# Loop 1 of a two-layer graph and mixture-of-experts kernel: S of two blocks by the two row halves of PE's array

## The chip, the cores and the metric

The kernel runs on one core of a Trainium2 chip. The metric is the time of one execution on the device, in microseconds; the runs are given by their median and their range. A second kind of execution is recorded by the hardware profiler, and all rows of a trace come from one such execution. Engines are called PE (TensorE), DVE (VectorE), ACT (ScalarE), POOL (GpSimd) and SP (the queue that issues most transfers).

## The reference

The input x has 5000 rows of 128; adj is a sparse 5000 x 5000 matrix of zeros and ones. Four steps follow one another, each with a layer norm ahead and a residual sum behind it. The first is the one that the change touches:

```
adj = A * (y @ y.T)                  # y: one-hot classes, 5000 x 16
row_l1 = maximum(sum(abs(adj), axis=1), 1e-12)
support = (adj / row_l1) @ input     # input = layernorm(x)
return 0.9 * support + 0.1 * h0
...
x = x + gnn0(layernorm(x)); x = x + moe0(layernorm(x))   # 8 experts, top 2, and a shared FFN
x = x + gnn1(layernorm(x)); x = x + moe1(layernorm(x))   # adj @ x and edge sums; 8 experts, top 2
```

The product y @ y.T is called S here. It is multiplied with adj, element by element, to give m.

## The kernel before

The 5000 nodes are padded to 5120, that is NB = 40 blocks of 128, or CH = 10 chunks of CW = 512 columns. Everything is ordered by hand: each engine runs its own program of nested loops over chunks k and steps s, and semaphores tie them together.

**Loop 1** (`a_iteration`, driven by `a_pipeline`) computes the first graph step, chunk by chunk. A chunk has STEPS = 43 steps. At step s of chunk k, for s below 40, PE multiplies block s of `ysta` (128 rows x 128, the stationary side) with the chunk's `ymov` (128 rows x 512) into one of two S banks, `sbank[s % 2]` (L726). DVE multiplies the bank with the adjacency block that lies in `ring` into `m` (L1561). Two steps later (LAG = 2) PE aggregates: `abank` += xn[b].T @ m[b] for b = s - 2 (L742), two instructions on PE since both sides are plain float32. ACT takes |m| into `mabs` (L1065), and once in four steps PE sums four such blocks by column quarters, `add_abs` (L790, 128 rows x 32 columns each); in chunks and loads named in PAIRS it does the same with edge products, `add_cols` (L800), after DVE made them (L1571). An S matmul waits until m of the block that last used its bank is made.

**y** has 16 classes. As float32 it is split into a high and a low part of type float32r, so that high x high, high x low, low x high and low x low give the full product. In `ysta` rows 0 to 63 hold two copies of the high part (32 rows each, of which 16 are zero), rows 64 to 127 two copies of the low part; `ymov` holds the 32-row groups in the order 0, 2, 1, 3. One contraction over 128 rows adds up all four products. `load_y` brings y in by 4 transfers for each piece, ACT makes the high part (`y_high_copy`, L959), DVE the low part on rows 64 to 127 (`y_low`, by `split_low`, L386), and `load_ymov` copies the chunk's columns from `ysta` to `ymov` by 4 transfers (L533). SP does that at the start of its loop for chunk k, that is behind the loads of chunk k-1.

**Beside these** PE runs, at fixed steps of a chunk, the transposes, router and ranks of the chunk before, and for chunks 2 to 8 the shared FFN of the chunk two before: `shared_up` at steps 2, 11, 20, 29 (three float32r matmuls into `ubank[n % 2]`, L665 to L667) and `shared_down` at steps 4, 13, 22, 31 (L680). ACT applies gelu between them.

SP loads the adjacency by 1 MB transfers of four blocks, in the order of LOAD_ORDER: `ring` slots 0, 1, 4 hold what S is multiplied with, the other slots the outgoing edges. Each load waits until its slot's last user is done. After loop 1 come the expert tiles, loop 2 (`z_iteration`, second graph step) and its expert tiles; they use the same PSUM banks, but nothing in them changes.

The eight PSUM banks are s0, s1, agg, u0, u1, d0, d1 and misc.

Of the kernel before, what the change touches and what calls it, by code (L numbers as in the profile page):

```python
# [8 lines left out]
ACT = mybir.ActivationFunctionType  # L9
# [7 lines left out]
P = 128  # L17
# [5 lines left out]
CLS = 16  # L23
# [12 lines left out]
GROUPS = P // 32  # L36

# [107 lines left out]
def bass_two_layer_gnn_moe_kernel(nc, x_t, adj_in, adj_out, h0_t, y_t, wr0, w1s, b1_0, w2s, b2_0,  # L145
# [144 lines left out]
    ubank = [psum("u0"), psum("u1")]  # L290
    dbank = [psum("d0"), psum("d1")]
# [179 lines left out]

    def beside(layer, s):

        i, q = divmod(s, TILE_STEPS[layer])
        return (layer * TILES + i if 0 <= i < BESIDE[layer] else None), q
# [26 lines left out]
    def _(sp):  # L502
# [26 lines left out]
        def load_ymov(k, buf):  # L529
            wait(sp, s_made, (k - 1) * NB)  # L530
            wait(sp, ymov_landed, 64 * k)
            for dst, src in enumerate((0, 2, 1, 3)):
                sp.dma_start(ymov[32 * dst:32 * dst + 32, buf, :].bitcast(F32),  # L533
                             ysta[32 * src:32 * src + 32, cols(k)].bitcast(F32)
                             ).then_inc(ymov_landed, 16)

        def load_y(first, last, landed):
# [3 lines left out]
            for g in range(4):  # L541
                sp.dma_start(dst[32 * g:32 * g + 32, :], y_t[:, first * YP:first * YP + n]).then_inc(landed, 16)
# [19 lines left out]
        for k in range(CH):  # L562
            if k:
                load_ymov(k, k % 2)
            for l in range(0 if k else 4, LOADS):
                load_next(2 if k and l in PAIRS[k] else 1)
# [85 lines left out]
    def _(pe):  # L652
# [5 lines left out]
        def shared_up(j, hb):  # L658
# [3 lines left out]
            wait(pe, ffn_gelu, n - 1)  # L662
            at, u = slice(hb * P, (hb + 1) * P), ubank[n % 2]
# [52 lines left out]

        def a_iteration(k, agg, mid, run_ffn):
            S, n = SA, width(k)
            for s in range(STEPS):
                if agg and s < NB:  # L720
                    if s == 0:
                        wait(pe, ymov_landed, 64 * (k + 1))
                    if isinstance(k, int) and k == 0 and s % Y_BLOCKS == 0:
                        pe.wait_ge(y_split, s // Y_BLOCKS + 1)
                    wait(pe, m_made, k * NB + s - 1)
                    pe.matmul(sbank[s % 2][:, 0:n], ysta[:, s * P:(s + 1) * P], ymov[:, k % 2, 0:n],  # L726
                              start=True, stop=True).then_inc(s_made, 1)
# [227 lines left out]
    def _(act):  # L955
        def y_high_copy(c):
            act.wait_ge(yraw_landed[min(c, 2)], 16 * 4)
# [125 lines left out]
        def shared_gelu(j, hb):  # L1083
# [4 lines left out]
            act.activation(h[:, n % H_BUFS, :], ubank[n % 2][:], ACT.Gelu, bias=b1[:, hb:hb + 1]).then_inc(ffn_gelu, 1)  # L1088
# [827 lines left out]
```

## Time and profile before

| what | us |
|---|---|
| median of 3 runs | 1473.44 |
| their range | 1466.86 to 1474.15 |
| span of the profiled execution, first to last instruction | 1555.4 |
| PE busy in it | 1367.5 (88%) |
| DVE busy | 929.2 (60%) |
| ACT busy | 649.6 (42%) |
| POOL busy | 461.5 (30%) |

For the profiled execution the span is the only time there is; it is longer than the runs without a profiler, so sums are made from its rows and then set against the median. Loop 1 reaches from about 13 us to about 735 us of the span. Start times in a row are from the span's start. Matmuls are pipelined: a row's duration has a modelled end, and two rows can overlap, so what an instruction costs PE is read from start to start. PEld rows are weight loads, which run beside the matmuls.

### The profile page before, as it was taken

The page shows a single profiled execution, that of the slowest core. Times are in us where ns is not written, and L with a number is a line of the kernel's source. Part 1 is how long each engine was busy: PE and PEld are TensorE (multiplying, and loading weights), DVE is VectorE, ACT ScalarE, POOL GpSimd, SP SyncE. Part 2 cuts the span into 40 slices and gives each one's busy share as a digit, 9 for nine tenths or more (in the row PEclk, how much of TensorE's full clock was granted, in tenths as well). Part 3 has the DMA queues.
Part 4 walks back from the last instruction along what each step waited for, and adds up shares of the span by engine and source line. Part 5 has one row for each costly group of instructions (what it writes and reads, how often), then busy time and mean ns, then how long its engine had stood idle before and what let it go on. Part 6 is the DMA issues. An engine that isn't in the chain of part 4 may idle for free.

```text
span 1555.4 us, 21717 instructions
## 1 busy us (share of the span) xinstructions
PE 1367.5 (88%) x6536; PEld 829.7 (53%) x6536; DVE 929.2 (60%) x2670; ACT 649.6 (42%) x1108; POOL 461.5 (30%) x450
## 2 busy tenths in 40 slices
PE   5998999999999999998689999999999998766771
PEld 2443444444444444456578877466666666545550
DVE  6775858576776767684322224777777777432224
ACT  3454344343444433444244344565555555422220
POOL 2102021111202020213545554223323332465652
PEclk9999999999999999999899999999999999978885
DMA  9688988696888787875366442889888888433435
GB/s 314 253 335 315 337 297 305 239 341 238 321 274 317 265 318 266 304 248 206 104 250 223 170 165 96 312 296 311 296 292 308 304 287 250 117 111 113 126 109 202
DMA packets 117360, 386.22 MB, mean 248 GB/s; under 512 B 20116, under 2 KB 49587, under 8 KB 87824
## 3 DMA queue, kind: packets, MB, share of 16 engines
q1 hardware_dynamic: 77296, 327.32, 60.9%
q10 hardware_dynamic: 27136, 33.93, 6.2%
q0 software_dynamic: 12832, 23.81, 4.3%
q8 instruction: 46, 0.75, 0.2%
q14 instruction: 50, 0.41, 0.1%
HBM read 332.80 MB, written 57.41 MB: 251 GB/s over the span
## 4 chain that ended last, share of the span: by engine, by line
PE 51%; issue 12%; DVE 10%; another core or an unknown queue 5%; ACT 4%; POOL 3%; DMA 2%; DVEq 0%; POOLq 0%; ACTq 0%; SPq 0%
PE agg L742 14%; PE d L846 7%; PE s L726 6%; PE d L790 4%; POOL rows_scratch L1798 3%; PE d L800 2%; PE d L680 2%; DVE adj_over_wb L386 2%; PE agg L913 2%; PE u L831 2%; PE u L833 2%; ACT h L1101 2%; PE u L827 1%; PE u L832 1%
## 5 line engine op out<-in xcount | busy, mean ns | idle before, releaser
L742 PE MATMUL agg<-m,xn 128*128 128x512 f32 (+1 forms) x800 | 399.4, 585 | 0.0
L1065 ACT ACTIVATE mabs<-m 128x512 f32<-128x512 f32 (+1 forms) x400 | 243.7, 619 | 322.4 <-DVE m L1561 289.4
L1561 DVE TENSOR_TENSOR m<-s,ring 128x512 f32<-128x512 f32 (+1 forms) x400 | 268.2, 676 | 184.2 <-PE s L726 127.7
L726 PE MATMUL s<-ymov,ysta 128*128 128x512 f32 (+1 forms) x400 | 244.8, 616 | 42.7 <-DVE m L1561 24.7
L1798 POOL DMA_INDIRECT rows_scratch<-xrow,idx x160 | 183.8, 1149 | 297.8 <-DVE xrow L1306 102.8
L1807 POOL DMA_INDIRECT y_scratch<-yo,ids x164 | 160.9, 981 | 138.9 <-DVE yo L1456 70.8
L742 PEld LDWEIGHTS agg<-m,xn 128*128 128x128 f32 x800 | 152.2, 191 | 62.8 <-issue 41.9
L726 PEld LDWEIGHTS s<-ymov,ysta 128*128 128x128 f32 x400 | 75.3, 190 | 199.7 <-issue 97.8
L386 DVE TENSOR_TENSOR adj_over_wb<-ring,adj_over_wb 128x512 fp32r<-128x512 f32 (+1 forms) x216 | 138.8, 672 | 48.5 <-ACT adj_over_wb L1165 44.7
L1784 POOL TENSOR_TENSOR rstd<-vareps,mhalf 128x4 f32<-128x4 f32 x30 | 38.3, 1277 | 405.6 <-DVE vareps L1218 405.6
L1165 ACT CAST adj_over_wb<-ring 128x512 fp32r<-128x512 f32 (+1 forms) x216 | 125.6, 607 | 45.7 <-PE agg L920 42.6
L913 PE MATMUL agg<-ring,xn 128*128 128x512 f32 (+1 forms) x260 | 126.3, 589 | 2.1 <-ACT xn L1142 2.0
L918 PE MATMUL agg<-adj_over_wb,ysta 128*128 128x512 f32 (+1 forms) x216 | 109.4, 506 | 16.3 <-DVE adj_over_wb L386 8.4
L1101 ACT ACTIVATE h<-u,wb 128x512 f32<-128x512 f32 x108 | 72.8, 686 | 117.4 <-PE u L833 101.0
L846 PE MATMUL d<-wb,h 128*128 128x128 f32 x864 | 112.0, 278 | 10.5 <-ACT h L1101 10.5
L846 PEld LDWEIGHTS d<-wb,h 128*128 128x128 f32 x864 | 108.8, 194 | 16.5 <-ACT h L1101 11.6
L790 PE MATMUL d<-mabs,picks 128*32 128x512 f32 (+1 forms) x800 | 106.7, 606 | 3.2 <-ACT mabs L1065 3.2
L846 PE MATMUL d<-wbz,h 128*128 128x128 f32 x432 | 65.9, 313 | 45.6 <-ACT h L1101 40.4
L1435 DVE TENSOR_TENSOR tile_x<-s,tile_x 128x512 fp32r<-128x512 f32 x27 | 18.7, 691 | 121.5 <-ACT tile_x L1094 76.1
L1571 DVE CUSTOM_DVE_ANT_0 ring<-ring 128x512 f32<-128x512 f32 (+1 forms) x132 | 88.4, 671 | 2.5 <-DMA ring<-in_adj_out 2.4
L846 PEld LDWEIGHTS d<-wbz,h 128*128 128x128 f32 x432 | 60.6, 222 | 50.4 <-DVE term L1443 32.3
L1101 ACT ACTIVATE h<-u,wbz 128x512 f32<-128x512 f32 x54 | 36.1, 686 | 117.9 <-remote 57.7
(242 smaller groups left out, 1982.8 us busy)
## 6 DMA issues: line engine op xcount, KB each, us to landing
ring<-in_adj_in SPq DMA_DIRECT2D x180, 1024.0 KB
ring<-in_adj_out SPq DMA_DIRECT2D x30, 1024.0 KB
wb<-blob_scratch SPq DMA_DIRECT2D x27, 834.0 KB
rows_scratch<-yo ACTq DMA_DIRECT2D x81, 260.0 KB, 6.7
stage<-in_adj_out SPq DMA_DIRECT2D x19, 1024.0 KB
ring<-in_adj_in SPq DMA_DIRECT2D x20, 784.0 KB
xt<-rows_scratch SPq DMA_DIRECT2D x54, 260.0 KB
wbz<-blob_scratch SPq DMA_DIRECT2D x27, 193.0 KB
```

Source lines behind the costliest of these rows:

```text
L386: return eng.tensor_tensor(low, raw, high.bitcast(F32), ALU.subtract)
L726: pe.matmul(sbank[s % 2][:, 0:n], ysta[:, s * P:(s + 1) * P], ymov[:, k % 2, 0:n], start=True, stop=True).then_inc(s_made, 1)
L742: pe.matmul(abank[:, 0:n], xn[:, b, :], m[:, b % M_BUFS, 0:n], start=b == 0, stop=b == NB - 1).then_inc(S["agg_blocks"], 1)
L790: last = pe.matmul(dbank[1][32 * i:32 * i + 32, 0:width(k)], pick[0], mabs[:, (g * GROUPS + i) % ABS_BUFS, 0:width(k)], start=g == 0, stop ...
L846: last = pe.matmul(dbank[t % 2][:, q * D:(q + 1) * D], h[:, n % H_BUFS, q * P:(q + 1) * P], tile_part(t, "down", hb), start=hb == 0 and q ...
L913: pe.matmul(abank[:, 0:n], xn[:, b, :], slot_part(l % 5, b % LB, n), start=b == 0, stop=b == NB - 1).then_inc(S["agg_blocks"], 1)
L1065: act.activation(mabs[:, b % ABS_BUFS, 0:width(k)], m[:, b % M_BUFS, 0:width(k)], ACT.Abs).then_inc(abs_made, 1)
L1101: act.activation(h[:, n % H_BUFS, :], ubank[n % 2][:], ACT.Gelu, bias=tile_part(t, "bias1", hb)).then_inc(tile_gelu, 1)
L1165: act.copy(adj_part(0, s)[:, 0:width(k)], slot_part(l % 5, s % LB, width(k))).then_inc(adj_high, 1)
L1561: dve.tensor_tensor(m[:, s % M_BUFS, 0:width(k)], sbank[s % 2][:, 0:width(k)], slot_part(LOAD_AT[k, l, False][0], s % LB, width(k)), ALU.m ...
L1798: pool.indirect_dma_start(out=rows_dram, out_offset=bass.IndirectOffsetOnAxis(ap=idx[:, t, c:c + 1], axis=0), in_=xrow[:, t, c, :], in_off ...
L1807: pool.indirect_dma_start(out=y_dram[layer], out_offset=bass.IndirectOffsetOnAxis(ap=ids[:, buf, q:q + 1], axis=0), in_=yo_part(t)[:, q, : ...
```

## The change

`ysta` and `ymov` now hold 16-row groups without the zeros: each half of 64 rows has two copies of the high part and two of the low part in `ysta`, and the matching order in `ymov`. So 64 rows give the whole of S, and the two halves can be given two different blocks. `two_products` issues both matmuls (`tile_size` 64 x 128, at rows 0 and 64) at even steps, into two of three banks: s0, s1 and u1. The first pair of a chunk is issued at step 40 of the chunk before; the other pairs at steps 2, 4, ... 38.

- y is loaded by 8 transfers for a piece instead of 4, `ymov` by 8 instead of 4; the bytes are the same.
- `ymov` of chunk k + 1 is loaded in chunk k, ahead of its load 5.
- The low part is made by two DVE instructions on 32 partitions each instead of one on 64.
- The early `shared_up` all use u0, and wait for the gelu just before.

The core of the diff:

```diff
+HALF = P // 2
+Y_COPIES = P // CLS
+YMOV_LANDED = 16 * Y_COPIES
...
+    s_turn = sbank + [ubank[1]]
...
+    def shared_up_bank(n):
+        return ubank[n % 2 if n >= LATER * HID[0] else 0]
...
         def load_ymov(k, buf):
             wait(sp, s_made, (k - 1) * NB)
-            wait(sp, ymov_landed, 64 * k)
-            for dst, src in enumerate((0, 2, 1, 3)):
-                sp.dma_start(ymov[32 * dst:32 * dst + 32, buf, :].bitcast(F32),
-                             ysta[32 * src:32 * src + 32, cols(k)].bitcast(F32)
-                             ).then_inc(ymov_landed, 16)
+            wait(sp, ymov_landed, YMOV_LANDED * k)
+            for dst in range(Y_COPIES):
+                src = dst // 4 * HALF + dst % 2 * 2 * CLS
+                sp.dma_start(ymov[CLS * dst:CLS * dst + CLS, buf, :].bitcast(F32),
+                             ysta[src:src + CLS, cols(k)].bitcast(F32)).then_inc(ymov_landed, 16)
...
-            for g in range(4):
-                sp.dma_start(dst[32 * g:32 * g + 32, :], y_t[:, first * YP:first * YP + n]).then_inc(landed, 16)
+            for g in range(Y_COPIES):
+                sp.dma_start(dst[CLS * g:CLS * g + CLS, :], y_t[0:CLS, first * YP:first * YP + n]).then_inc(landed, 16)
...
         for k in range(CH):
-            if k:
-                load_ymov(k, k % 2)
             for l in range(0 if k else 4, LOADS):
+                if l == 5 and k + 1 < CH:
+                    load_ymov(k + 1, (k + 1) % 2)
...
-            wait(pe, ffn_gelu, n - 1)
-            at, u = slice(hb * P, (hb + 1) * P), ubank[n % 2]
+            wait(pe, ffn_gelu, n if j < LATER else n - 1)
+            at, u = slice(hb * P, (hb + 1) * P), shared_up_bank(n)
...
+        def two_products(k, s):
+
+            if s == 0:
+                wait(pe, ymov_landed, YMOV_LANDED * (k + 1))
+            if k == 0 and s % Y_BLOCKS == 0:
+                pe.wait_ge(y_split, s // Y_BLOCKS + 1)
+            wait(pe, m_made, k * NB + s - 1)
+            for i in range(2):
+                rows, b = slice(i * HALF, (i + 1) * HALF), s + i
+                pe.matmul(s_turn[(k * NB + b) % 3][:, 0:width(k)], ysta[rows, b * P:(b + 1) * P],
+                          ymov[rows, k % 2, 0:width(k)], start=True, stop=True).then_inc(s_made, 1)
...
-                if agg and s < NB:
-                    if s == 0:
-                        wait(pe, ymov_landed, 64 * (k + 1))
-                    if isinstance(k, int) and k == 0 and s % Y_BLOCKS == 0:
-                        pe.wait_ge(y_split, s // Y_BLOCKS + 1)
-                    wait(pe, m_made, k * NB + s - 1)
-                    pe.matmul(sbank[s % 2][:, 0:n], ysta[:, s * P:(s + 1) * P], ymov[:, k % 2, 0:n],
-                              start=True, stop=True).then_inc(s_made, 1)
+                if k == 0 and s == 0:
+                    two_products(0, 0)
+                if agg and s % 2 == 0 and 2 <= s < NB:
+                    two_products(k, s)
+                if agg and s == NB and k + 1 < CH:
+                    two_products(k + 1, 0)
...
-            split_low(dve, ysta[64:128, at], raw[64:128, :], ysta[64:128, at]).then_inc(y_split, 1)
+            for first in (2 * CLS, HALF + 2 * CLS):
+                low = slice(first, first + 2 * CLS)
+                last = split_low(dve, ysta[low, at], raw[low, :], ysta[low, at])
+            last.then_inc(y_split, 1)
```

How the instructions stand. First PE in chunk 0, steps 4 to 8, before; s is an S bank, agg the aggregate's, d1 takes the sums of four blocks:

```order
L742 MATMUL agg<-m,xn 128x512
L726 MATMUL s1<-ymov,ysta 128x512
L742 MATMUL agg<-m,xn 128x512
L726 MATMUL s0<-ymov,ysta 128x512
L742 MATMUL agg<-m,xn 128x512
L790 MATMUL d1<-mabs,picks 32x512 x4
L726 MATMUL s1<-ymov,ysta 128x512
L742 MATMUL agg<-m,xn 128x512
```

The same place on PE afterwards; L733 is an S matmul on half the rows, L759 the aggregate, L807 the sums:

```order
L759 MATMUL agg<-m,xn 128x512 x2
L733 MATMUL s0<-ymov,ysta 128x512
L733 MATMUL s1<-ymov,ysta 128x512
L759 MATMUL agg<-m,xn 128x512
L807 MATMUL d1<-mabs,picks 32x512 x4
L759 MATMUL agg<-m,xn 128x512
L733 MATMUL u1<-ymov,ysta 128x512
L733 MATMUL s0<-ymov,ysta 128x512
```

Two S stand together between full-size matmuls, two agg behind each pair, and the sums lie between two agg where an S followed them before.

Second, PE where one chunk ends and the next begins, before; the second row of sums belongs to step 42:

```order
L742 MATMUL agg<-m,xn 128x512 x3
L790 MATMUL d1<-mabs,picks 32x512 x4
L726 MATMUL s0<-ymov,ysta 128x512
L726 MATMUL s1<-ymov,ysta 128x512
L726 MATMUL s0<-ymov,ysta 128x512
L665 MATMUL u0<-xnfh,ws1h 128x512
L666 MATMUL u0<-xnfl,ws1h 128x512
L667 MATMUL u0<-xnfh,ws1l 128x512
L742 MATMUL agg<-m,xn 128x512
```

And afterwards, the same chunk's end:

```order
L733 MATMUL s1<-ymov,ysta 128x512
L733 MATMUL u1<-ymov,ysta 128x512
L759 MATMUL agg<-m,xn 128x512 x2
L807 MATMUL d1<-mabs,picks 32x512 x4
L733 MATMUL s0<-ymov,ysta 128x512
L733 MATMUL s1<-ymov,ysta 128x512
L672 MATMUL u0<-xnfh,ws1h 128x512
L673 MATMUL u0<-xnfl,ws1h 128x512
```

The first two rows are blocks 0 and 1 of the next chunk, now ahead of the last two agg of this one; behind the sums stands the pair (2, 3).

Third, SP at the start, before:

```order
L542 DMA h<-in_y_t 32x1024 x4
L504 DMA xres<-in_x_t 128x1280
L518 DMA ring<-in_adj_in 128x2048
L542 DMA stage<-in_y_t 32x1024 x4
L533 DMA ymov<-ysta 32x512 x4
```

and afterwards:

```order
L549 DMA h<-in_y_t 16x1024 x8
L511 DMA xres<-in_x_t 128x1280
L525 DMA ring<-in_adj_in 128x2048
L549 DMA stage<-in_y_t 16x1024 x8
L541 DMA ymov<-ysta 16x512 x8
```

Nothing is in another place, but twice as many issues stand ahead of the first S.

## Rows read from the trace of the kernel before

**Rows 1.** The page: busy time, and the span in 40 slices, in tenths.

```profile
PE 1367.5 (88%) x6536; PEld 829.7 (53%) x6536; DVE 929.2 (60%) x2670; ACT 649.6 (42%) x1108; POOL 461.5 (30%) x450
...
PE   5998999999999999998689999999999998766771
```

**Rows 2.** Busy us by stretch of loop 1; then granted clock, DMA share, GB/s.

```profile
20.00:95.00 75.00, 69.22 (x257) 28.60 (x256) 59.19 (x178) 32.49 (x53) 6.62 (x4) 0.98 0.84 301
...
250.00:330.00 80.00, 76.97 (x351) 36.91 (x350) 54.08 (x149) 30.98 (x53) 10.80 (x11) 0.98 0.78 283
```

**Rows 3.** Waits between 95 and 700 us: total us, times, longest.

```profile
PE s L726 <- DVE m L1561: 21.1, 23, 2.6
...
DVE m L1561 <- PE s L726: 113.8, 116, 3.5
```

**Rows 4.** PE and weight loads in order: start us, us, instruction, idle before.

```profile
456.98 0.42 PEld L742 LDWEIGHTS agg<-m,xn 128*128 128x128 f32 x2 [0.24 <-issue]
457.21 1.02 PE L742 MATMUL agg<-m,xn 128*128 128x512 f32 x2
...
458.30 1.02 PE L742 MATMUL agg<-m,xn 128*128 128x512 f32 x2
...
459.25 1.07 PE L790 MATMUL d<-mabs,picks 128*32 128x512 f32 x8
...
460.13 1.04 PE L800 MATMUL d<-stage,picks 128*32 128x512 f32 x8
...
461.10 0.19 PEld L726 LDWEIGHTS s<-ymov,ysta 128*128 128x128 f32 x1 [0.84 <-DVE m L1561]
461.10 0.50 PE L726 MATMUL s<-ymov,ysta 128*128 128x512 f32 x1
461.21 0.19 PEld L665 LDWEIGHTS u<-xnfh,ws1h 128*128 128x128 f32 x1
461.44 0.40 PE L665 MATMUL u<-xnfh,ws1h 128*128 128x512 f32 x1
...
461.68 0.39 PE L666 MATMUL u<-xnfl,ws1h 128*128 128x512 f32 x1
...
461.90 0.40 PE L667 MATMUL u<-xnfh,ws1l 128*128 128x512 f32 x1
```

**Rows 5.** PE in order, where an S follows abs directly.

```profile
467.24 1.07 PE L790 MATMUL d<-mabs,picks 128*32 128x512 f32 x8
468.24 0.50 PE L726 MATMUL s<-ymov,ysta 128*128 128x512 f32 x1
```

**Rows 6.** PE, then DVE, in order at the start of chunk 6.

```profile
442.95 0.73 PE L726 MATMUL s<-ymov,ysta 128*128 128x512 f32 x2
444.29 0.50 PE L726 MATMUL s<-ymov,ysta 128*128 128x512 f32 x1 [0.61 <-DVE m L1561]
...
443.55 1.29 DVE L1561 TENSOR_TENSOR m<-s,ring 128x512 f32<-128x512 f32 x2 [2.40 <-issue]
```

**Rows 7.** All engines in order, the first 13 us: y's way to S.

```profile
0.81 1.80 SPq L542 DMA_DIRECT2D h<-in_y_t  x4
...
6.53 1.22 DVE L386 TENSOR_TENSOR ysta<-h,ysta 64x1024 fp32r<-64x1024 f32 x1 [5.11 <-ACT ysta L959]
7.78 2.52 SPq L533 DMA_DIRECT2D ymov<-ysta  x4
...
12.85 1.22 PE L726 MATMUL s<-ymov,ysta 128*128 128x512 f32 x2 [12.85 <-DMA ymov<-ysta]
```

**Rows 8.** SP, DVE and PE in order around 271 to 282 us (chunk 3).

```profile
271.52 2.52 SPq L533 DMA_DIRECT2D ymov<-ysta  x4
281.18 0.33 SPq L518 DMA_DIRECT2D ring<-in_adj_in  x1
...
279.86 0.69 DVE L1561 TENSOR_TENSOR m<-s,ring 128x512 f32<-128x512 f32 x1 [3.82 <-issue]
...
280.60 0.79 PE L726 MATMUL s<-ymov,ysta 128*128 128x512 f32 x1 [2.42 <-DVE m L1561]
```

More of the change, by code:

```diff
@@ L956, in y_high_copy @@
         def y_high_copy(c):
-            act.wait_ge(yraw_landed[min(c, 2)], 16 * 4)
+            act.wait_ge(yraw_landed[min(c, 2)], YMOV_LANDED)
             raw, at = y_piece(c)
@@ L1087, in shared_gelu @@
             wait(act, ffn_down, n + 1 - H_BUFS)
-            act.activation(h[:, n % H_BUFS, :], ubank[n % 2][:], ACT.Gelu, bias=b1[:, hb:hb + 1]).then_inc(ffn_gelu, 1)
+            act.activation(h[:, n % H_BUFS, :], shared_up_bank(n)[:], ACT.Gelu, bias=b1[:, hb:hb + 1]).then_inc(ffn_gelu, 1)
         def tile_high_part(t):
@@ L1560, in a_iteration @@
                     wait(dve, abs_made, k * NB + s + 1 - M_BUFS)
-                    dve.tensor_tensor(m[:, s % M_BUFS, 0:width(k)], sbank[s % 2][:, 0:width(k)],
+                    dve.tensor_tensor(m[:, s % M_BUFS, 0:width(k)], s_turn[(k * NB + s) % 3][:, 0:width(k)],
                                       slot_part(LOAD_AT[k, l, False][0], s % LB, width(k)), ALU.mult).then_inc(m_made, 1)
```

## The prediction

> **What bounds the kernel now.** I read the page first: PE is busy 88% of the span, and its row of slices stands at 8 or 9 from the second slice to the eighteenth, where loop 1 runs [rows 1]. The table by stretch then says that in loop 1 the granted clock is 0.98, that DVE is busy 59.19 of 75 us early and 54.08 of 80 us later, and that the DMA engines are at 0.78 to 0.84 [rows 2]. So nothing but PE is full. "Busy" does not yet say that PE streams without a gap, so I read the waits: between 95 and 700 us the S matmul waited for DVE 21.1 us in 23 waits, while DVE waited for that matmul 113.8 us [rows 3]. PE leads, DVE follows.
>
> Then start-to-start times on PE. With nothing else between, one agg starts 1.09 us after the other (457.21, 458.30), and that holds one S and one agg [rows 4]. The three matmuls of the shared FFN have S's size and type, and start 0.24 and 0.22 us apart [rows 4]; I take S at 0.23 and an agg (two instructions) at 0.86. The durations printed beside them are longer because ends are modelled.
>
> **The pair itself.** Two S cost 2 x 0.23 = 0.46 us now. Afterwards the two halves of PE's rows work side by side, so one stream of 0.23 could hold both. The trace has no matmul on half the rows, but it has matmuls on a quarter of the columns (abs and cols, 128*32), and they show two things. They do run side by side: eight of them, four quarters and two passes each, take 0.88 us (459.25 to 460.13) [rows 4], no more than the two passes of one agg. And PE pays at the change of tile shape: an agg before abs takes 0.95 instead of 0.86, so 0.09 us going in; cols before an S takes 0.97 instead of 0.88 (460.13 to 461.10), and abs before an S 1.00 (467.24 to 468.24), so 0.09 to 0.12 coming out [rows 4, 5]. The S behind it takes 0.34 instead of 0.23 (461.10 to 461.44), because its weights are no longer loaded under the matmul before: its weight load starts with it, and the next weight load 0.11 later (461.10, 461.21) [rows 4]. In the same shape a weight load starts about 0.23 us ahead of its agg, under the S in flight (456.98 against 457.21) [rows 4].
>
> I price the change from full rows to half rows and back by these. A pair then costs 0.09 (in) + 0.11 (its weights) + 0.01 (the second half behind the first, as abs's quarters do) + 0.23 (stream) + 0.10 (out) + 0.11 (weights of the agg behind it) = 0.65 us. That is 0.19 more than the two S that it replaces. The bounds: below, the change of shape is free and a pair costs 0.23, which is -0.23; above, the second half's weights load after the first's (+0.11, so +0.30), and at worst the halves do not overlap (another 0.23, so +0.53). I take +0.19, since the column rows are the nearest there are, and both shapes use the same array. Where S stood behind abs, an agg now stands there and pays the same on leaving the column shape: no gain.
>
> The Trainium skill's page TensorEngine Tiling (Array Packing), section Key Properties, says that changing the tiling mode, not merely the tile, drains TensorE. The 0.09 us before abs agrees with that. Its section Theoretical Speedup promises up to 2x for a contraction of 64 or fewer, which by itself would be the free case; the rival below weighs that.
>
> The sum on PE: chunks 1 to 8 have 160 pairs, x 0.19 = +30.4. Chunk 9 is 392 columns wide, where S streams 0.23 x 392/512 = 0.18: a pair is 0.60 against 0.36, +0.24 x 20 = +4.8. In chunk 0 PE is busy less (69.22 of 75 us against 76.97 of 80) and DVE more [rows 2], so I count half of 20 x 0.19: +1.9. Together +37.1.
>
> **A chunk's first two S one chunk early.** At the start of chunk 6, S(0) and S(1) go at 442.95, take 0.34 + 0.23 and are done streaming at 443.52; S(2) needs a bank that DVE has yet to read, and starts at 444.29: PE stands 0.77 us. DVE had stood 2.40 us before its first m [rows 6]. With S(0), S(1) issued at step 40 of the chunk before, m(0) is long made when the pair (2, 3) comes. Nine chunk starts x 0.77 = -6.9. Chunk 0 keeps its own. Late next there would be the copy of the absolute sums (term) behind cols, needed at step 3; a pair, three up matmuls and two agg (0.65 + 0.69 + 1.72 = 3.1 us) lie between, ample for an ACT copy.
>
> **The start.** S(0) of chunk 0 starts at 12.85 us, released by the landing of ymov [rows 7]. The way there is serial: y's loads by SP, ACT's cast, DVE's split, ymov's loads. SP issues h's four in 1.80 us, so four more are +1.8; the split is 1.22 us on 64 partitions and becomes two on 32 each, +1.2 if time goes by elements per partition; ymov's four take 2.52, so four more +2.5 [rows 7]. Sum +5.5 with nothing beside it, since m and agg both need S. The bound below is 4.3, if half-height splits take half the time each. The four later splits fall into chunk 0's DVE stream, +4.9 us of DVE time where it is busy 79% [rows 2]; I count half, +2.5, bounds 0 and 4.9.
>
> **What is near nothing.** ymov for the next chunk is now issued by SP behind the loads of step 4 instead of step 9, and takes 8 issues, 5.0 us instead of 2.52. SP stands idle at DVE's pace anyway: after ymov (271.52 + 2.52 = 274.04) it issued the next adjacency load only at 281.18 [rows 8]. That idle time hides the 2.5 us more; uncovered, it would cost up to 2.5 x 9. The third S bank is u1, so every early up matmul waits for the gelu just before it; ups are nine steps apart and that gelu is done at once: nothing.
>
> **What already waits takes some of it.** In chunk 3 DVE waits 3.82 us with no releaser shown, at a block where a ring slot's load is first used, and PE then waits 2.42 us for DVE [rows 8]. Such a wait comes from a load, not from PE's pace, so a slower PE eats into it. Of the 21.1 us [rows 3] about 8 x 0.61 belongs to chunk starts, which leaves 16; I take -4, with 0 and -12 as bounds.
>
> **The sum.** 37.1 - 6.9 + 5.5 + 2.5 - 4.0 = +34.2 us. The profiled execution spans 1555.4 us and the median of the runs is 1473.44; the matmul times hold at full clock in either, so I add the sum unscaled: 1508 us, 2.3% slower.
>
> **The rivals.**
> Free change of shape: PE switches from full rows to half rows without standing, and weights load underneath. A pair costs 0.23, PE gains 0.23 x 200 = 46 us. DVE and the loads become the bound in part (DVE at 54 to 59 us of 75 to 80), so perhaps half of what the waits now hold comes back as new waits, +13. With -6.9 + 5.5 + 2.5: about -32, 1441 us. It decides from a pair of 0.46 downward: below that the change gains. For it speaks that quarter tiles, once in their shape, overlap perfectly; against it the 0.09 and 0.12 us at every border of the column shape [rows 4, 5]. By the skill's Theoretical Speedup this would be the outcome.
> Half exposed: PE stands at the border but the weights of both halves, or of the agg behind, load under what runs. A pair costs 0.09 + 0.23 + 0.10 + 0.01 = 0.43; -6 on 200 pairs, -6.9, +8.0: 1468 us, within what can be told from no change.
> Serial weights: the two halves load one after the other, 0.76 a pair: +22 to the sum, 1530 us.
> No overlap: the halves run one after the other, so that the change does not do what it says: 0.88 a pair, +46, with more of the waits absorbed 1550 us.
> DVE starved instead: against that, two S are ready at once in three banks, and m(s-1) is there for DVE while PE makes the pair; I give it no case of its own.
>
> **Chances.** Forecast 0.56; serial weights 0.10; no overlap 0.06; free 0.13; half exposed 0.15. A difference of 0.5%, about 7 us, is what a measurement of this kernel can tell from none. Faster: the free case and a quarter of the half exposed, 0.17. Same: most of the rest of half exposed, 0.10. Slower: 0.73. Around the forecast alone the unknown costs give 1490 to 1525. For 8 in 10 I leave out no overlap, the outer part of serial weights and most of the free case: 1450 to 1534.
>
> **What would show it.** In the changed kernel's PE rows: agg to first S 0.95 instead of 0.86; the second S of a pair starting about 0.01 us behind the first (0.11: serial; 0.23: no overlap); from first S to the agg behind it about 0.35 plus the wait to leave, against 0.63 for two S. The time over a stretch of pairs and agg without abs should be 0.65 + 2 x 0.86 = 2.37 us per two blocks, against 2.18. A chunk of 512 columns should grow by 20 x 0.19 - 0.77 = 3.0 us, less what its waits take, the first S move from 12.85 to about 18.4, and the wait before a chunk's S(2) be gone. I am wrong if two blocks take less than 2.18 us there, or if PE's share is not what sets a chunk's time, so that idle before agg grows or shrinks by what the pairs add.

## The result: 1.6% slower, and what the profile of the changed kernel shows

| kernel | median, us | range | ratio to before (95% interval) |
|---|---|---|---|
| before | 1471.78 | 1466.86 to 1474.15 | |
| changed | 1494.22 | 1492.92 to 1494.82 | 1.0155 (1.0133 to 1.0177) |
| changed, measured a second time, against a kernel before of 1472.46 | 1498.56 | 1497.56 to 1499.02 | 1.0177 (1.0150 to 1.0204) |

The change costs 22 to 26 us. The forecast was 1508 us, slower by 34: the direction and the mechanism on PE came out as forecast, the size was two thirds to three quarters of it. The page of the changed kernel, answering to [rows 1]: its span, the busy times, the slices.

```profile
span 1492.3 us, 21774 instructions
...
PE 1363.6 (91%) x6536; PEld 771.4 (52%) x6536; DVE 928.9 (62%) x2675; ACT 649.9 (44%) x1108; POOL 465.5 (31%) x450
...
PE   3999899999999999999999999999999999998940
```

The span is 1492.3 us and fits the runs. That of the kernel before did not: the execution profiled there spanned 1555.4 us against 1472 in the runs. A second trace of the kernel before, taken with the experiments, spans 1471.7 us, and from here on "before" is that trace. Of the 83.7 us that the first one is longer, 17 lie in loop 1.

PE at the end of chunk 5 of the changed kernel, in order (start us, us, instruction, idle before), its second trace, which spans 1495.8 us and is meant by "changed" from here on; this answers to [rows 4]:

```profile
438.90 0.50 PE L733 MATMUL u<-ymov,ysta 64*128 64x512 f32 x1
438.91 0.49 PE L733 MATMUL s<-ymov,ysta 64*128 64x512 f32 x1
439.33 1.99 PE L759 MATMUL agg<-m,xn 128*128 128x512 f32 x4
441.25 0.49 PE L733 MATMUL s<-ymov,ysta 64*128 64x512 f32 x1
441.25 0.50 PE L733 MATMUL u<-ymov,ysta 64*128 64x512 f32 x1
441.68 1.13 PE L759 MATMUL agg<-m,xn 128*128 128x512 f32 x2
442.73 1.07 PE L807 MATMUL d<-mabs,picks 128*32 128x512 f32 x8
443.62 1.04 PE L817 MATMUL d<-stage,picks 128*32 128x512 f32 x8
444.59 1.13 PE L759 MATMUL agg<-m,xn 128*128 128x512 f32 x2
445.64 0.50 PE L733 MATMUL s<-ymov,ysta 64*128 64x512 f32 x2
```

The two halves start within 0.01 us of one another and the next matmul starts 0.43 us after the first (438.90 to 439.33): they do run side by side. The two agg behind them (x4) take 1.92 us to the next pair (439.33 to 441.25) where two agg cost 1.72. So a pair costs 0.43 + 0.20 = 0.63 us in place of 0.46 for two S, and two blocks go round in 2.35 us (438.90 to 441.25). The weight loads of the same places:

```profile
438.90 0.18 PEld L733 LDWEIGHTS u<-ymov,ysta 64*128 64x128 f32 x1 [0.76 <-issue]
438.90 0.18 PEld L733 LDWEIGHTS s<-ymov,ysta 64*128 64x128 f32 x1
439.33 0.30 PEld L759 LDWEIGHTS agg<-m,xn 128*128 128x128 f32 x2 [0.24 <-issue]
```

The weights of both halves are loaded at the same time, and only when PE has changed its shape; the agg's weights start with the agg (439.33 for both) and no longer 0.23 us ahead of it. The loader stands for 0.76 us before the pair. In the same place with full rows (the experiment full_rows below) it stands 0.24:

```profile
530.91 0.19 PEld L733 LDWEIGHTS u<-ymov,ysta 128*128 128x128 f32 x1 [0.24 <-issue]
```

The waits between 95 and 690 us, answering to [rows 3]: first before, then changed (total us, times, longest).

```profile
PE s L726 <- DVE m L1561: 13.9, 16, 4.5
```

```profile
PE u L733 <- DVE m L1581: 3.1, 2, 2.4
PE s L733 <- DVE m L1581: 1.8, 1, 1.8
PE agg L759 <- DVE m L1581: 0.5, 1, 0.5
```

PE waits for DVE 5.4 us instead of 13.9; 4.8 of the difference are the eight waits of 0.6 at chunk starts. It is freed of waits and loses more than that at the borders of its shape.

Where the time stands, from the starts of each chunk's first agg in the two traces:

| stretch | before | changed | difference |
|---|---|---|---|
| start to first agg of chunk 1 | 82.3 | 89.7 | +7.4 |
| chunk 1 | 62.1 | 62.9 | +0.8 |
| chunk 2 | 79.7 | 80.2 | +0.5 |
| chunks 3 to 8 | 421.9 | 433.1 | +11.2 |
| chunk 9, to its last agg | 50.4 | 52.8 | +2.4 |
| all that follows | 775.3 | 777.1 | +1.8 |

The sum is 24.1 us, as much as the spans differ (1471.7 and 1495.8). The first stretch is the least certain: it is 80.6 us in the longer trace of before, and 91.7 in the first trace of the changed kernel.

### The profile page after: what moved, and what is told of

Same layout as the page of the kernel before. It is cut to its first block, busy times and chain, and to the rows that moved or that the text cites. A ratio compares the mean times of both kernels' runs of the same rounds, so it can differ in the third digit from the quotient of the medians.

```text
span 1492.3 us, 21774 instructions
## 1 busy us (share of the span) xinstructions
PE 1363.6 (91%) x6536; PEld 771.4 (52%) x6536; DVE 928.9 (62%) x2675; ACT 649.9 (44%) x1108; POOL 465.5 (31%) x450
## 4 chain that ended last, share of the span: by engine, by line
PE 57%; DVE 11%; issue 9%; POOL 5%; ACT 3%; DMA 3%; DVEq 0%; POOLq 0%; SPq 0%; ACTq 0%
PE agg L759 19%; PE d L863 6%; PE d L807 5%; POOL y_scratch L1827 4%; PE agg L930 3%; PE s L733 3%; PE d L817 2%; DVE adj_over_wb L390 2%; PE d L687 2%; PE agg L935 2%; PE agg L936 2%; PE agg L937 2%; PE u L848 2%; PE u L733 1%; POOL rows_scratch L1818 1%
## 5 line engine op out<-in xcount | busy, mean ns | idle before, releaser
L759 PE MATMUL agg<-m,xn 128*128 128x512 f32 (+1 forms) x800 | 418.7, 623 | 0.5 <-DVE m L1581 0.5
L1581 DVE TENSOR_TENSOR m<-s,ring 128x512 f32<-128x512 f32 (+1 forms) x267 | 177.9, 673 | 116.5 <-PE s L733 45.3
L759 PEld LDWEIGHTS agg<-m,xn 128*128 128x128 f32 x800 | 129.8, 190 | 158.5 <-issue 94.0
L1581 DVE TENSOR_TENSOR m<-u,ring 128x512 f32<-128x512 f32 (+1 forms) x133 | 89.6, 674 | 67.9 <-PE s L733 33.9
L935 PE MATMUL agg<-adj_over_wb,ysta 128*128 128x512 f32 (+1 forms) x216 | 109.1, 505 | 16.7 <-DVE adj_over_wb L390 9.3
L733 PE MATMUL s<-ymov,ysta 64*128 64x512 f32 (+1 forms) x267 | 99.7, 498 | 20.4 <-DMA ymov<-ysta 16.3
L807 PE MATMUL d<-mabs,picks 128*32 128x512 f32 (+1 forms) x800 | 106.1, 602 | 6.2 <-ACT mabs L1082 6.2
L733 PEld LDWEIGHTS s<-ymov,ysta 64*128 64x128 f32 x267 | 37.2, 185 | 96.2 <-issue 52.1
L937 PE MATMUL agg<-adj_over_wb,xnl 128*128 128x512 f32 (+1 forms) x216 | 83.8, 388 | 0.0
L936 PE MATMUL agg<-adj_over_wb,ysta 128*128 128x512 f32 (+1 forms) x216 | 83.7, 388 | 0.0
```

The costliest lines, as they stand in the source:

```text
L733: pe.matmul(s_turn[(k * NB + b) % 3][:, 0:width(k)], ysta[rows, b * P:(b + 1) * P], ymov[rows, k % 2, 0:width(k)], start=True, stop=True). ...
L759: pe.matmul(abank[:, 0:n], xn[:, b, :], m[:, b % M_BUFS, 0:n], start=b == 0, stop=b == NB - 1).then_inc(S["agg_blocks"], 1)
L807: last = pe.matmul(dbank[1][32 * i:32 * i + 32, 0:width(k)], pick[0], mabs[:, (g * GROUPS + i) % ABS_BUFS, 0:width(k)], start=g == 0, stop ...
L935: pe.matmul(abank[:, 0:n], xnh[:, b, :], hi, start=b == 0, stop=False)
L1581: dve.tensor_tensor(m[:, s % M_BUFS, 0:width(k)], s_turn[(k * NB + s) % 3][:, 0:width(k)], slot_part(LOAD_AT[k, l, False][0], s % LB, widt ...
```

## The experiments

The times of each are set beside the kernel before on the same chip, whose median was 1472.4 to 1473.3 us each time. Two theories stood against each other: the border between full rows and half rows on PE (S), or the doubled transfers and splits of y (L).

**The changed kernel again**, as the one with which its variants are compared.

> The changed kernel once more, on the chip on which its variants run. Theory S (the border between full and half rows): PE pays about 0.17 us a pair, 200 pairs, +34 us, against which stand the early first pair (-7) and the slower start and chunk 0 (about +4 to +11). Rival L (the layout): the doubled transfers and the doubled split at the start and in chunk 0 are most of the loss. Both expect 1494 us here.

1498.56 us (1497.56 to 1499.02).

**Full rows.** Only PE's shape goes back:

```diff
-                rows, b = slice(i * HALF, (i + 1) * HALF), s + i
+                rows, b = slice(0, P), s + i
```

> The changed kernel with one edit: both S matmuls of a pair use all 128 rows, so PE never leaves its full shape for them; order, banks, transfers and splits stay. S comes out doubled, which the division by the row sums takes out again. Theory S: two S cost 0.46 us instead of 0.63, 34 us less, so about 1460 us, below the kernel before. Rival L: the shape is cheap and the time stays within 5 us of 1494.

1472.56 us (1469.86 to 1475.02), ratio 0.9998 (0.9984 to 1.0011) to the kernel before: 26.0 us less than the changed kernel, which gives back the whole loss. Two successive chunk starts, by the first agg of chunks 7 and 8, changed kernel first, then full rows:

```profile
523.00 1.02 PE L759 MATMUL agg<-m,xn 128*128 128x512 f32 x2
...
594.94 0.59 PE L759 MATMUL agg<-m,xn 128*128 128x512 f32 x1
```

```profile
506.58 0.59 PE L759 MATMUL agg<-m,xn 128*128 128x512 f32 x1
...
575.72 0.59 PE L759 MATMUL agg<-m,xn 128*128 128x512 f32 x1
```

71.94 against 69.14 us: half rows cost 2.80 us a chunk. Theory S had the mechanism and promised 34 us, 8 too many; L's "within 5 us of 1494" is out.

**Full rows and the old layout of y**: 4 transfers of 32 rows, one split, S by full rows as in full_rows.

```diff
-Y_COPIES = P // CLS
+Y_COPIES = 4
...
-                src = dst // 4 * HALF + dst % 2 * 2 * CLS
-                sp.dma_start(ymov[CLS * dst:CLS * dst + CLS, buf, :].bitcast(F32),
-                             ysta[src:src + CLS, cols(k)].bitcast(F32)).then_inc(ymov_landed, 16)
+                src = (0, 2, 1, 3)[dst]
+                sp.dma_start(ymov[32 * dst:32 * dst + 32, buf, :].bitcast(F32),
+                             ysta[32 * src:32 * src + 32, cols(k)].bitcast(F32)).then_inc(ymov_landed, 16)
...
-                sp.dma_start(dst[CLS * g:CLS * g + CLS, :], y_t[0:CLS, first * YP:first * YP + n]).then_inc(landed, 16)
+                sp.dma_start(dst[32 * g:32 * g + 32, :], y_t[:, first * YP:first * YP + n]).then_inc(landed, 16)
...
-            for first in (2 * CLS, HALF + 2 * CLS):
-                low = slice(first, first + 2 * CLS)
-                last = split_low(dve, ysta[low, at], raw[low, :], ysta[low, at])
-            last.then_inc(y_split, 1)
+            split_low(dve, ysta[64:128, at], raw[64:128, :], ysta[64:128, at]).then_inc(y_split, 1)
```

> As full_rows, and y in the old layout too (32-row groups, 4 transfers, one split on 64 partitions). What is left of the change: S in pairs at even steps by full rows, three banks, the first pair one chunk early, ymov loaded earlier. Theory S: a further 4 to 10 us less than full_rows, 1450 to 1457 us, the first S at 12.9 us instead of 16.3. Rival L: with S's shape not at fault, going back to the old layout is what helps, full_rows near 1494 and this one near the 1472 of the kernel before.

1463.68 us (1461.27 to 1466.48), ratio 0.9942 (0.9924 to 0.9961): 8.9 us below full_rows, and 0.6% faster than the kernel before, the best of all kernels here. So the change holds a gain (the order) and two losses (the shape, 26 us; the layout, 9 us). The layout's 9 us lie ahead of chunk 1: its first agg starts at 80.0 us here and at 87.9 in full_rows, and from there both need the same time, 69.1 us for chunk 7.

**No early pair**: a chunk's first pair at step 0 of its own chunk.

```diff
-                if k == 0 and s == 0:
-                    two_products(0, 0)
-                if agg and s % 2 == 0 and 2 <= s < NB:
+                if agg and s % 2 == 0 and s < NB:
                     two_products(k, s)
-                if agg and s == NB and k + 1 < CH:
-                    two_products(k + 1, 0)
```

> The changed kernel with one edit: a chunk's first pair is issued at step 0 of its own chunk, not at step 40 of the one before. Theory: PE stands about 0.77 us or more at each of nine chunk starts again, +7 us, 1501 us. Rival: DVE or the loads set the chunk's start anyway, and the time stays within 2 us of 1494.

1500.93 us (1498.25 to 1502.38), 2.4 us more than the changed kernel, a third of what was expected; the ranges of the two overlap. Chunks 7 and 8 by their first agg:

```profile
524.44 0.59 PE L755 MATMUL agg<-m,xn 128*128 128x512 f32 x1
...
597.08 0.59 PE L755 MATMUL agg<-m,xn 128*128 128x512 f32 x1
```

72.64 us a chunk against 71.94: the early pair gives 0.70 us here, close to the 0.77. The two traces differ by only 0.7 us in their spans (1496.5 and 1495.8), because chunk 2 goes the other way: it takes 76.9 us in this kernel and 80.2 in the changed one. Two things differ there. DVE waits for a store of the experts' weights, 5.2 us in the changed kernel (first row) and 3.8 in no_early (second), and PE then stands 2.4 and 1.4 us for DVE:

```profile
DVE wlow L390 <- DMA blob_scratch<-wlow: 5.2, 1, 5.2
```

```profile
DVE wlow L390 <- DMA blob_scratch<-wlow: 3.8, 1, 3.8
```

And the granted clock falls to half as that stand of PE ends in the changed kernel, for 6.8 us in all, and not in no_early. All of chunk 2 and five of those 6.8 us in the changed kernel, then all of chunk 2 in no_early (stretch, us, busy times, granted clock, DMA share, GB/s):

```profile
152.60:232.80 80.20, 75.96 (x326) 29.83 (x325) 54.71 (x152) 30.68 (x51) 10.78 (x11) 0.96 0.86 317
161.00:166.00 5.00, 5.00 (x16) 1.32 (x20) 4.93 (x15) 1.81 (x3) 0.00 (x0) 0.50 0.14 55
```

```profile
154.50:231.40 76.90, 72.86 (x326) 29.38 (x324) 54.46 (x152) 30.18 (x50) 10.77 (x11) 1.00 0.89 326
```

6.8 us at half clock are worth at most 3.4 us, as much as the whole difference (an estimate, from the 6.8); the shorter stand is worth 1.0. Executions of one kernel differ in this too: the first trace of the changed kernel has 3.4 us at half clock in chunk 2 and takes 79.1 us for it. So what took the rest of the expected 7 us was not isolated, by these traces the clock more than the store.

**The same without the half rows**: old_layout_full with the early pair taken out by the same edit.

> old_layout_full (full rows, old layout, pairs, three banks; 1464 us) with a chunk's first pair at step 0 of its own chunk. Theory: the early pair is what makes old_layout_full faster than the kernel before; each of nine chunk starts costs 0.7 us again, of which the wait for the weights' low parts in chunk 2 hides two or three, so +3 to +5 us, 1468. Rival: the gain comes from S standing in pairs or from three banks, and the time stays at 1464.

1470.00 us (1466.45 to 1473.70), ratio to before 0.9990 (0.9977 to 1.0004): 6.3 us more than old_layout_full. Full-size chunks 3 to 8 take 0.8 to 0.9 us more each. So the early first pair makes the larger part of the gain over the kernel before, 6.3 of 8.8 us. Pairs, a third bank and the earlier load of ymov together are worth 2.6 us by the medians, which is not clear of zero.

**One split**: full rows, the low parts together on rows 64 to 127.

```diff
-                src = dst // 4 * HALF + dst % 2 * 2 * CLS
+                src = dst % 2 * HALF
...
-            for first in (2 * CLS, HALF + 2 * CLS):
-                low = slice(first, first + 2 * CLS)
-                last = split_low(dve, ysta[low, at], raw[low, :], ysta[low, at])
-            last.then_inc(y_split, 1)
+            split_low(dve, ysta[HALF:P, at], raw[HALF:P, :], ysta[HALF:P, at]).then_inc(y_split, 1)
```

> full_rows (1472.6 us) with the low parts together on rows 64 to 127, so that DVE splits a piece by one instruction again; the 8 transfers of 16 rows for y and ymov stay. Theory: the second split is 1.2 us for each of five pieces and explains most of the 9 us between full_rows and old_layout_full, so 1466 to 1467, the first S at about 15 us, chunk 0 some 4 us shorter. Rival: the transfers' issues on SP do it, and the time stays within 2 us of 1472.

1470.37 us (1467.49 to 1474.02), 2.2 us below full_rows, with ranges that overlap: the theory, 6 us, fell. The first S starts at 15.70 us instead of 16.26, but the first agg of chunk 1 at 87.8, as in full_rows (87.9). The second split is not what chunk 0 loses.

**Sums beside the pair**: abs and cols (`sums` calls `add_abs` and `add_cols` as before) directly behind the pair, so that PE goes from half rows to column quarters without the full shape between.

```diff
                 if agg and s == NB and k + 1 < CH:
                     two_products(k + 1, 0)
+                if agg and 6 <= s < NB and s % GROUPS == 2:
+                    sums(k, s // GROUPS - 1)
...
-                if agg and s >= 6 and s % GROUPS == 2:
-                    l = s // GROUPS - 1
-                    if l < LOADS - 1:
-                        add_abs(k, l)
-                    if l in PAIRS[k] and l != k:
-                        add_cols(k, l)
-                    if l == LOADS - 1:
-                        add_abs(k, l)
+                if agg and s == NB + 2:
+                    sums(k, LOADS - 1)
```

> The changed kernel with one edit: the sums of four blocks (abs, cols) stand directly behind the pair, ahead of the aggregate, in steps 6 to 38. PE then goes full, half rows, column quarters, full instead of full, half rows, full, column quarters, full: one border and one uncovered weight load less, nine times a chunk. Theory S: 0.17 to 0.20 us each, 90 times, 15 to 18 us less than 1498. Rival: PE now waits there for ACT's and DVE's results of a block just made, and the time stays at 1498 or rises.

1481.84 us (1480.90 to 1482.26), ratio 1.0074 (1.0050 to 1.0097) to before and 16.7 us below the changed kernel, inside the 15 to 18. PE there:

```profile
404.72 1.02 PE L761 MATMUL agg<-m,xn 128*128 128x512 f32 x2
405.67 0.50 PE L733 MATMUL s<-ymov,ysta 64*128 64x512 f32 x2
406.10 1.06 PE L812 MATMUL d<-mabs,picks 128*32 128x512 f32 x8
407.10 1.12 PE L761 MATMUL agg<-m,xn 128*128 128x512 f32 x2
```

The pair still takes 0.43 us (405.67 to 406.10), but the agg that stood between it and the sums, with its border of 0.09 and its uncovered weights of 0.11, now pays neither. A border removed gives back about what it was priced at (0.09 + 0.11): 16.7 us for 90 borders, 0.19 each, and in chunk 7 1.83 us for nine, 0.20 each (71.94 against 70.11).

**One transfer for each load of y**, on the changed kernel and, with 4 copies of 32 rows, on old_layout_full ("best"):

```diff
-            for g in range(Y_COPIES):
-                sp.dma_start(dst[CLS * g:CLS * g + CLS, :], y_t[0:CLS, first * YP:first * YP + n]).then_inc(landed, 16)
+            src = y_t[0:CLS, first * YP:first * YP + n]
+            sp.dma_start(dst, src.unsqueeze(0).to_broadcast([Y_COPIES, CLS, n])).then_inc(landed, 16)
...
-            act.wait_ge(yraw_landed[min(c, 2)], YMOV_LANDED)
+            act.wait_ge(yraw_landed[min(c, 2)], 16)
```

> The changed kernel with one edit: each of the three pieces of y comes by one transfer that reads the 16 rows eight times, instead of 8 transfers. SP then has 21 issues fewer, 0.46 us each, 9.7 us, ahead of chunk 0's loads; ymov keeps its 8, DVE its two splits. Theory P (SP's issues are what chunk 0 loses): the first S at about 13 us instead of 16.3, chunk 0 some 4 us shorter, in all 7 to 8 us less, about 1491. Rival D (DVE's second split and its place in DVE's order): at most the 3 us of the start, 1496.

> old_layout_full (1463.7 us: full rows in pairs, first pair early, old layout) with each piece of y by one transfer instead of 4. SP has 9 issues fewer, 4 us. Theory P: the first S 1.4 us earlier and the loads of chunk 0 up to 4 us earlier, so 1460 to 1462. Rival D: the start is bound by the landing of the data, and the time stays at 1463 to 1464. Either way below the kernel before by 0.5 to 0.9%.

1509.25 us (1502.89 to 1510.11), 11 us more than the changed kernel, and 1495.05 us (1493.03 to 1498.31), 31 us more than old_layout_full. Both theories were wrong: SP issued less, and the time rose. SP did not even get ahead: it had to wait for the first piece, and issued ymov's first load at 13.35 us instead of 9.85. ACT's copies of the three first pieces, each waiting for its transfer, in the changed kernel and then in one_transfer, and the first one in best:

```profile
6.22 1.04 ACT L976 CAST ysta<-h 128x1024 fp32r<-128x1024 f32 x1 [4.13 <-DMA h<-in_y_t]
14.05 1.04 ACT L976 CAST ysta<-stage 128x1024 fp32r<-128x1024 f32 x1 [6.79 <-DMA stage<-in_y_t]
38.41 1.04 ACT L976 CAST ysta<-stage 128x1024 fp32r<-128x1024 f32 x1 [9.54 <-DMA stage<-in_y_t]
```

```profile
9.72 1.04 ACT L976 CAST ysta<-h 128x1024 fp32r<-128x1024 f32 x1 [7.63 <-DMA h<-in_y_t]
18.39 1.04 ACT L976 CAST ysta<-stage 128x1024 fp32r<-128x1024 f32 x1 [7.62 <-DMA stage<-in_y_t]
50.85 1.04 ACT L976 CAST ysta<-stage 128x1024 fp32r<-128x1024 f32 x1 [18.42 <-DMA stage<-in_y_t]
```

```profile
13.83 1.04 ACT L976 CAST ysta<-h 128x1024 fp32r<-128x1024 f32 x1 [11.74 <-DMA h<-in_y_t]
```

Four or eight copies in one transfer land later than as four or eight transfers: with eight the first piece is there at 9.72 us instead of 6.22, with four at 13.83 instead of 5.43 (old_layout_full). The first S starts at 19.84 us in one_transfer and at 28.00 in best. While PE, DVE and ACT all stand for y's third load in these two kernels, the DMA engines are a quarter busy in best (first row) and half busy in one_transfer (second; granted clock, DMA share and GB/s stand last):

```profile
50.00:58.00 8.00, 0.00 (x0) 0.00 (x0) 0.00 (x0) 0.00 (x0) 0.00 (x0) 0.50 0.26 78
```

```profile
47.00:50.50 3.50, 0.00 (x0) 0.00 (x0) 0.00 (x0) 0.00 (x0) 0.00 (x0) 0.50 0.49 131
```

The Trainium skill's page DMA: Bandwidth & Descriptors, section Why a DMA increments its semaphore by 16 and not by 1, says that a DMA is shared out over the largest number of engines up to 16 that divides the slowest dimension of both sides. On the source's side that dimension is the number of copies here, 8 or 4. The traces agree: 4 copies land later than 8, and the shares of 0.26 and 0.49 are those of 4 and 8 engines of 16.

**Every second transfer of y by ACT**, on the changed kernel and on old_layout_full ("best2"); each transfer stays as it was:

```diff
+    def load_y(eng, part, first, last, landed):
...
+        for g in range(part, Y_COPIES, 2):
+            eng.dma_start(dst[CLS * g:CLS * g + CLS, :], y_t[0:CLS, first * YP:first * YP + n]).then_inc(landed, 16)
...
+                    if s == 0:
+                        load_y(act, 1, 2, Y_PIECES, yraw_landed[2])
...
+        load_y(act, 1, 0, 1, yraw_landed[0])
         y_high_copy(0)
+        load_y(act, 1, 1, 2, yraw_landed[1])
```

> The changed kernel with its 24 transfers of y shared out: every second one is issued by ACT, which is idle at the start, each transfer as it was. SP has 12 issues fewer, 0.46 us each, 5.5 us, before chunk 0's loads; the way each transfer runs is the same, unlike in one_transfer, where the one transfer landed 7 us later than the eight. Theory P (SP's issues are what chunk 0 loses): first S at 14.4 instead of 16.3 us, and in all 4 to 7 us less than 1498.6, about 1493. Rival D (DVE's work in chunk 0): at most the 2 us of the start, 1496.5.

> old_layout_full (1463.7 us: full rows in pairs, first pair early, old layout) with every second transfer of y issued by ACT. SP has 6 issues fewer, 2.8 us. Theory P: 1 to 3 us less, 1461 to 1463. Rival D: the start hangs on the landing of the data, no change, 1463.7. Either way about 0.6 to 0.8% below the kernel before.

1497.53 us (1496.15 to 1497.76), 1.0 us less than the changed kernel, and 1468.30 us (1466.28 to 1469.77), 4.6 us more than old_layout_full. Fewer issues on SP gave nothing back. That does not price the issues by themselves, since the landings moved too: in y_by_act the first S starts at 20.95 us, where 14.4 was expected and the changed kernel has 16.29, and the last issue of y's third load ends at 18.60 us instead of 21.04, while ACT finds it landed at 40.01 instead of 38.41.

**What chunk 0 waits for.** The traces that were made for the wrong theories answer it together. ACT copies y's third piece (the first of its third load, which brings three) inside its queue of chunk 0, at step 8. While that load has not landed, |m| behind it is not made; PE's sums need that |m|, and DVE may not write the next of its four m buffers. PE's stand in the kernel before and in the changed one:

```profile
33.38 1.93 PE L790 MATMUL d<-mabs,picks 128*32 128x512 f32 x8 [3.15 <-ACT mabs L1065]
```

```profile
40.04 1.94 PE L807 MATMUL d<-mabs,picks 128*32 128x512 f32 x8 [6.30 <-ACT mabs L1082]
```

The third copy in the kernel before and in old_layout_full:

```profile
31.75 1.04 ACT L959 CAST ysta<-stage 128x1024 fp32r<-128x1024 f32 x1 [5.86 <-DMA stage<-in_y_t]
```

```profile
30.77 1.04 ACT L976 CAST ysta<-stage 128x1024 fp32r<-128x1024 f32 x1 [6.17 <-DMA stage<-in_y_t]
```

In the table, the last column is how much of the time between the two was granted at half clock, by the clock records of the trace.

| kernel | third copy starts | first agg of chunk 1 | between | at half clock |
|---|---|---|---|---|
| old_no_early | 30.27 | 78.0 | 47.7 | 0.0 |
| old_layout_full | 30.77 | 80.0 | 49.2 | 6.8 |
| before | 31.75 | 82.3 | 50.6 | 6.8 |
| best2 | 34.88 | 84.3 | 49.5 | 6.8 |
| sums_beside | 38.20 | 89.1 | 50.9 | 5.2 |
| one_split | 38.31 | 87.8 | 49.5 | 8.0 |
| changed | 38.41 | 89.7 | 51.3 | 6.1 |
| full_rows | 38.47 | 87.9 | 49.4 | 5.0 |
| changed, first trace | 38.47 | 91.7 | 53.2 | 10.2 |
| no_early | 39.26 | 90.8 | 51.6 | 5.9 |
| y_by_act | 40.01 | 92.1 | 52.1 | 6.8 |
| one_transfer | 50.85 | 101.4 | 50.6 | 4.6 |
| best | 63.45 | 111.5 | 48.1 | 5.1 |

Over 33 us of difference in the landing, the rest of chunk 0 stays at 47.7 to 50.6 us with full rows and at 50.6 to 53.2 with half rows. Take off half of the time at half clock, and it is 45.5 to 47.7 us with full rows and 48.1 to 48.7 with half rows. The first S does not lead in this way: in y_by_act it starts 4.7 us later than in the changed kernel, and chunk 1 only 2.4. That the landing leads is a reading of thirteen traces; no run changed the place of that copy alone, so it is well supported and not tested by itself.

## Why the prediction was right, step by step

**PE is the bound, DVE follows.** Right. PE was given 0.63 instead of 0.46 us a pair and the chunks grew.

**The pair, term by term.** Forecast 0.65, measured 0.63, where the two S before cost 0.46. The second half starts 0.00 to 0.01 us behind the first (0.01), its weights do not come one after the other (serial weights is out), the halves overlap (no overlap is out), PE stands at the borders and loads weights uncovered (free and half exposed are out). Two blocks were to take 2.37 us and take 2.35. The column quarters were a good stand-in for a shape of which the trace had no row.

**The sum over the pairs was too high.** Forecast 3.8 us for a full chunk (20 x 0.19), measured 2.80 (full rows against half rows, chunk 7). Laying the starts of agg in chunk 7 of the two kernels side by side, the gap between them grows by 0.16 to 0.17 us for each of 16 pairs, 2.6 us together, where the forecast had 0.19: that is about 0.4 of the difference. At four places it grows by 0.08 or less, and that is the other 0.6: the pair (2, 3), the pair at step 4 behind small matmuls (L780), the pair at step 20 beside an up matmul, and the one at step 26 behind the small rank matmuls (L707 to L712). For (2, 3) the rows tell why. Changed kernel, start of chunk 6:

```profile
448.87 1.04 PE L807 MATMUL d<-mabs,picks 128*32 128x512 f32 x8
449.84 0.50 PE L733 MATMUL u<-ymov,ysta 64*128 64x512 f32 x1
449.85 0.50 PE L733 MATMUL s<-ymov,ysta 64*128 64x512 f32 x1
450.27 0.50 PE L672 MATMUL u<-xnfh,ws1h 128*128 128x512 f32 x1
```

It stands directly behind the sums, so its border going in is the one that the sums pay coming out anyway, which sums_beside then showed for every fourth step. I had multiplied by 20 without looking at what stands before each pair in the order. For the other three places the reason was not tested.

**The early first pair.** Forecast -0.77 a chunk, measured -0.70 (no_early, changed) and -0.8 to -0.9 with full rows. The wait before S(2) is gone: in the rows above the pair starts 0.97 us after the sums, and the up matmul 0.43 us behind. As a sum, the runs show 6.3 us with full rows and the old layout, near the 6.9, and 2.4 in the changed kernel, where the two ranges overlap. There a sooner chunk start lengthened DVE's wait for the store in chunk 2, by which PE stood 1.0 us longer, and the traces also differ by 6.8 us at half clock, up to 3.4 us, for which the forecast had no term.

**The start and chunk 0.** Forecast +5.5, +2.5 and +1.9, together +9.9; measured +7.4 to chunk 1. The 1.9 for the shape was right: half rows against full rows 1.8 (89.7 and 87.9). Of the other 8.0, for which 5.6 were measured (full rows against before, 87.9 and 82.3), the mechanisms were wrong, and that the size came near is luck. The first S moved from 14.69 to 16.29 us (from 12.85 in the longer trace of before), not by 5.5. The issues and splits grew as forecast (h's issues take 3.65 us for 1.80, ymov's 5.04 for 2.52, the two splits 2.45 for 1.22), but they do not simply add up: S started 7.2 us after SP began to issue ymov in the kernel before, 5.1 in its longer trace, and 6.4 in the changed kernel, so the longer issue was mostly hidden. The four later second splits were to cost 2.5 in chunk 0 and cost nothing there (one_split: 87.8 for 87.9). What costs is the third load of y: its last issue ends at 21.04 us instead of 14.17, and ACT finds it landed at 38.41 instead of 31.75.

**What already waits.** Forecast -4, from a wait of 3.82 us at block 32 [rows 8]. In the second trace of before, PE waits 13.9 us for DVE in all that stretch and not 21.1, and no chunk from 3 on waits at block 32. This term rested on an execution 5.6% longer than the runs, which was visible at the time. Its size came out all the same, by luck: outside the chunk starts PE's waits fell from 9.1 to 5.4 us, more than half of that in chunk 2, where the longest wait follows the store and not a load of the ring.

**The sum.** By the same traces, forecast first:

| term | forecast | measured |
|---|---|---|
| the shape, less the waits that it takes up | 37.1 - 4.0 = 33.1 | 1.8 + 23.2 = 25.0 |
| order and banks, chunks 1 to 9 | -6.9 | -8.2 |
| start and later splits | +8.0 | +5.6 |
| behind loop 1 | 0 | +1.8 |
| sum | 34.2 | 24.2 |

The shape is half rows against full rows (1.8 us in chunk 0; 629.04 and 605.87 us for chunks 1 to 9), order and banks are full rows against before (605.87 and 614.11). So 8.1 of the 10 us that the forecast was too high are the shape's, multiplied by 20 places of which four cost little. What follows loop 1 was to be unchanged and is 1.8 us longer in the traces; the two traces of the changed kernel differ there by more (772.6 and 777.1). The stated range, 1450 to 1534 us, reached from 23 us faster to 61 slower and would have held most outcomes; what speaks for the forecast is the pair, 0.63 us for 0.65, and the two blocks, 2.35 for 2.37. The growth of a full chunk, 3.0 us less what its waits take, was too high: chunk 7 grew by 2.0 (69.96 to 71.94).

## What to carry to other kernels

Half of PE's rows for a short contraction is no gain by itself: it has to be set against the changes of shape around it. Here one pair of 0.23 us streams stood between two changes that cost 0.20 us each with their uncovered weights, and lost. Placed where PE leaves its full shape anyway, one change in every four steps fell away and gave 16.7 us back; more than one pair between two changes was not tried. Before a term is multiplied by a count, read in the order what stands before each of the places; and when a profiled span is longer than the runs, take its stalls as suspect; its start-to-start times held here (0.46 for two S, 1.72 for two agg). When two traces differ in one stretch, look at the granted clock there before naming a cause.

## What the runs showed of the hardware that I had not expected

- One transfer that reads 16 rows eight times lands its 512 KB 3.5 us later than eight transfers of 64 KB (9.72 against 6.22 us), one that reads 32 rows four times 8.4 us later than four transfers of 128 KB (13.83 against 5.43): fewer issues are not a faster transfer.
- PE's matmuls on two halves of its rows, with 128 columns each into two banks, start within 0.01 us and take 0.43 us until the next matmul, a full one (438.90 to 439.33) or column quarters (405.67 to 406.10): from half rows straight to column quarters costs no more than from half rows to full.
- The border has the same price for rows as for columns: an agg ahead of a pair or of the sums takes 1.05 us with uncovered weights in both cases (441.68 to 442.73, 444.59 to 445.64).
- Towards the end of PE's stand in chunk 0 the granted clock fell to half: it is 0.50 from 33 to 39 us in the kernel before (a stand of 3.15 us, up to 33.38) and from 38 to 44 us in the changed one (6.30, up to 40.04). The eight sums that follow took 1.93 and 1.94 us, where the same eight take 1.07 in chunk 5.
